# Scan layer in another order on four engines, and an attention stage that looks for shares before the turned rows

## The reference

```python
x = L0_attn_x
xn = _layernorm(x)
x = x + attention(xn) * _silu(expert_choice_ffn(xn))      # 32 experts, 8 tokens each per batch
xn = _layernorm(x)
# selective scan, 512 channels, 16 states
xc, z = split((xn @ fc1_w.T + fc1_b) @ in_proj_w.T)
u = _silu(causal_conv4(xc) + conv_b)
dt_low, Bm, Cm = split(u @ x_proj_w.T)
dt = softplus(dt_low @ dt_proj_w.T + dt_proj_b)
def step(hstate, t):
    dA = jnp.exp(dt_t[..., None] * A)
    hstate = dA * hstate + (dt_t * u_t)[..., None] * B_t[:, None, :]
    y_t = jnp.einsum('bdn,bn->bd', hstate, C_t)
    return (hstate, y_t)
s = ((y + u * D) * _silu(z)) @ out_proj_w.T @ fc2_w.T + fc2_b
# gated network, hidden 768, weights whole numbers over 127
g = _silu((_silu(xn @ wg.T) * (xn @ wu.T)) @ wd.T)
return x + s * g
```

## Time and profile before

| | |
|---|---|
| median of three runs | 2787.99 us (2785.57 to 2789.45) |
| the profiled execution, its own time | 2788.2 us |
| its span, first to last instruction | 2786.4 us |
| mean granted TensorE clock | 0.966 |
| busy in the span | PE 2542.0, DVE 2333.8, ACT 2011.2, POOL 2013.2 us |
| scan layer, start to start of a tile's first step input | 107.4, then 13 times 116.0 to 116.3, then 115.3 us |

### The profile page before, as it was taken

One profiled execution on the slowest core, in us unless ns is written; L12 is line 12 of the kernel. 1 busy time (PEld: TensorE's weight loads), 2 busy tenths in 40 slices (PEclk: granted clock), 3 DMA queues, 4 the chain that ended last, 5 costly groups with the idle time before them and its releaser, 6 DMA issues. The chain is left out here.

```text
span 2786.4 us, 37406 instructions
## 1 busy us (share of the span) xinstructions
PE 2542.0 (91%) x13454; PEld 1490.8 (54%) x13454; DVE 2333.8 (84%) x2899; ACT 2011.2 (72%) x3253; POOL 2013.2 (72%) x682
## 2 busy tenths in 40 slices
PE   7897899999976799999999999999999999999988
PEld 3454344443443465656656566565655656556565
DVE  7685777777733899898998989989899898998996
ACT  4222466666643798897988979889798897988974
POOL 0656011111211999999999999999999999999996
PEclk9898999999978799999999999999999999999999
DMA  6337999888541231321313213132131321313210
GB/s 188 116 116 179 260 218 236 205 200 224 211 161 49 105 130 29 117 92 46 130 26 119 92 46 130 25 120 92 46 130 24 121 92 46 130 24 114 92 46 8
DMA packets 121586, 316.00 MB, mean 113 GB/s; under 512 B 15517, under 2 KB 76445, under 8 KB 104878
## 3 DMA queue, kind: packets, MB, share of 16 engines
q1 hardware_dynamic: 91210, 233.32, 27.3%
q0 software_dynamic: 27888, 79.24, 10.3%
q10 hardware_dynamic: 2304, 1.05, 0.2%
HBM read 278.89 MB, written 43.13 MB: 116 GB/s over the span
## 5 line engine op out<-in xcount | busy, mean ns | idle before, releaser
L1523 DVE TENSOR_TENSOR_SCAN l_st<-l_p_a,l_hl,l_st 128x512 f32<-128x512 f32 x768 | 930.2, 1263 | 90.5 <-ACT l_p_a L1808 83.3
L1721 POOL TENSOR_TENSOR l_st<-l_st,lw_cs 128x2048 f32<-128x2048 f32 x192 | 878.4, 4634 | 3.2 <-ACT l_hl L1813 3.2
L1808 ACT ACTIVATE l_p_a<-l_dt,lw_a_neg 128x512 f32<-128x512 f32 x1024 | 666.5, 681 | 67.2 <-DVE keep_xg L1523 41.1
L1713 POOL TENSOR_TENSOR l_st<-l_bs,l_dtu 128x2048 f32<-128x2048 f32 (+1 forms) x128 | 555.1, 4337 | 57.2 <-PE l_p_y L2098 53.3
L2098 PEld LDWEIGHTS l_p_y<-keep_ident,l_st 128*128 128x128 f32 x3072 | 355.1, 145 | 118.6 <-issue 73.0
L2098 PE MATMUL l_p_y<-keep_ident,l_st 128*128 128x128 f32 x3072 | 380.5, 281 | 28.7 <-POOL l_st L1721 28.7
L1020 ACT ACTIVATE a_pr<-a_p_s 128x512 f32<-128x512 f32 x512 | 284.7, 596 | 143.8 <-PE a_p_s L1089 140.0
L931 DVE TENSOR_REDUCE a_mpart<-a_p_m 128x1 f32<-128x512 f32 x512 | 312.0, 679 | 12.2 <-PE a_p_m L1045 11.0
L1523 DVE TENSOR_TENSOR_SCAN keep_xg<-l_p_a,l_hl,keep_xg 128x512 f32<-128x512 f32 x256 | 314.5, 1265 | 1.6
L1721 POOL TENSOR_TENSOR keep_xg<-keep_xg,lw_cs 128x2048 f32<-128x2048 f32 x64 | 299.7, 4682 | 2.0 <-ACT l_hl L1813 2.0
L858 POOL DMA_DIRECT2D a_w<-in_w_dram x32 | 23.1, 737 | 327.2 <-PE a_p_m L1119 271.3
(11 more groups left out here) (246 smaller groups left out, 4007.9 us busy)
## 6 DMA issues: line engine op xcount, KB each, us to landing
l_bs<-s_bc SPq DMA_DIRECT2D x64, 1024.0 KB, 4.7
lw_cs<-s_bc SPq DMA_DIRECT2D x64, 1024.0 KB, 4.7
a_w<-in_w_dram POOLq DMA_DIRECT2D x32, 1024.0 KB, 12.0
late<-in_w_dram POOLq DMA_DIRECT2D x32, 1024.0 KB, 19.4
kx<-s_kp SPq DMA_DIRECT2D x96, 256.0 KB, 12.3
s_kp<-late SPq DMA_DIRECT2D x96, 128.0 KB, 2.1
s_vp<-late SPq DMA_DIRECT2D x16, 544.0 KB, 3.5
a_vg<-s_vp SPq DMA_DIRECT2D x16, 544.0 KB, 14.8
```

The source lines that it names most:

```text
L1523: eng.tensor_tensor_scan(st[k % NG][:, n, :], p_a[:, n, :], st[k % NG][:, n, :], hl[:, k, n:n + 1], ALU.mult, ALU.add).then_inc(scan_ok, 1)
L1713: eng.tensor_tensor(st[n][:, first:NG, :], bs[:, 4 * n + first:4 * n + 4, :], dtu[(k // NG) % 2][:, :].unsqueeze(1).broadcast_to([P, NG - ...
L1721: eng.tensor_tensor(st[n][:, :, :], st[n][:, :, :], cs[:, 4 * n:4 * n + 4, :], ALU.mult).then_inc(cm_ok, 1)
L1808: eng.activation(p_a[:, n, :], dt[c % 2][:, :], ACT.Exp, scale=a_neg[:, c, m:m + 1]).then_inc(dA_ok, 1)
```

## The change

**Attention.** The call of `one_choice` moves in front of the wait for the turned rows, still behind the maxima.

```diff
                     maxima(g, b, hg)
+                    if g == HG:
+                        eng.wait_ge(consts, 16 * 4)
+                    if g >= HG:
+                        one_choice(g - HG, b - 1, hg)
                     if hg % 2:
                         eng.wait_ge(hTp_ok, q + 1)
...
                     if g == 0:
                         return
-                    if g == HG:
-                        eng.wait_ge(consts, 16 * 4)
-                    if g >= HG:
-                        one_choice(g - HG, b - 1, hg)
                     take(*prev(g, b, hg))
```

```diff
-                 ("op", 0, END, 0), ("dt", 2, SCAN, 1), ("op", 1, END, 1), ("cv", 0, FRONT, 0), ("z", 0, SCAN, 1),
...
+        FILLS = (("tr", 1, FRONT, 1), ("dn", 1, END, 0), ("yb", 3, END, 1), ("xc", 0, FRONT, 0), ("op", 0, END, 1),
+                 ("xc", 1, FRONT, 0), ("z", 0, SCAN, 1), ("dt", 2, SCAN, 0), ("z", 1, SCAN, 0), ("op", 1, END, 1),
```

GpSimd:

```diff
                     if end:
+                        weighed(f, 11)
+                        weighed(f, 12)
                         dbu(f, 15)
+                        weighed(f, 13)
                     if scan:
                         step_input(s, o, 0)
...
                     if scan:
+                        weighed(s, 0)
                         step_input(s, o, 1)
-                        weighed(s, 0)
                         dbu(s, 3)
                         weighed(s, 1)
                         weighed(s, 2)
                         dbu(s, 5)
                         weighed(s, 3)
-                        step_input(s, o, 2)
-                    if end and f < NT - 1:
-                        residual(f)
-                    if scan:
                         weighed(s, 4)
                         dbu(s, 7)
                         weighed(s, 5)
+                        step_input(s, o, 2)
+                    if end:
+                        residual(f)
+                    if scan:
+                        dbu(s, 9)
                         weighed(s, 6)
-                        dbu(s, 9)
                         weighed(s, 7)
```

TensorE's and ScalarE's ends of a period, and the first tile:

```diff
-                    if q == 0:
-                        keep_busy(12, p_w[:, 0, :])
...
+                        up_h(q, s, o, 3)
+                        up_h(q, s, o, 4)
+                        sums(s, 14)
+                        up_h(q, s, o, 5)
+                    if front:
+                        step_low(q, q, 1)
+                    if scan:
+                        down(q, s, 0)
+                        sums(s, 15)
+                    if nxt:
+                        turn(q, q + 1, 0)
```

```diff
                     if front:
                         step_input(q, 0)
                     if scan:
-                        exp_unit(s, 15, 2)
+                        gate_z(s, 3)
+                        gate_h(s, 5)
+                    if nxt:
+                        normed(q + 1)
+                    if scan:
+                        exp_tables()
                         exp_unit(s, 15, 3)
                     if front:
                         exp_unit(q, 0, 0)
                         exp_unit(q, 0, 1)
-                    if scan:
-                        gate_z(s, 3)
-                    if front:
-                        exp_tables()
                         exp_unit(q, 0, 2)
+                        exp_unit(q, 0, 3)
```

More of the change, by code:

```diff
@@ L1506, in first_conv @@
                     taken(eng, "tr", 0, 1)
-                    wait(eng, done["cv"], c - 1)
+                    wait(eng, done["cv"], max([x + 1 for x in range(c) if bank("cv", x) == bank("cv", c)], default=0))
                     taken(eng, "xc", 0, c)
@@ L1911, in period @@
                         step_log(s, 1)
+                        exp_unit(s, 1, 0)
                         exp_unit(s, 1, 1)
+                        last(s, 0)
                         exp_unit(s, 1, 2)
                         exp_unit(s, 1, 3)
+                    if end:
+                        gate_out(f, 0)
                     if front:
@@ L1968, in period @@
                         exp_unit(s, 6, 2)
-                        step_input(s, 2)
-                        last(s, 5)
                         exp_unit(s, 6, 3)
                         exp_unit(s, 7, 0)
+                        last(s, 5)
+                        summed(s, 0)
+                        exp_unit(s, 7, 1)
+                    if front:
+                        conv_out(q, p, 0)
+                    if scan:
+                        exp_tables()
+                        exp_unit(s, 7, 2)
+                        exp_unit(s, 7, 3)
+                        step_log(s, 3)
+                        step_input(s, 2)
                     if front:
@@ L2050, in period @@
                         exp_unit(s, 14, 3)
+                        last(s, 13)
+                    if front:
+                        step_log(q, 0)
+                    if q == 0:
+                        norm_scale(1)
+                    if scan:
                         gate_h(s, 4)
-                        last(s, 13)
-                        gate_h(s, 5)
-                        summed(s, 2)
-                        gate_z(s, 2)
                         exp_tables()
@@ L2228, in period @@
                     if end:
+                        back(q, f, p, 3)
+                    if front:
+                        conv_in(q, q, p, 0)
+                    if scan:
+                        sums(s, 1)
+                    if end:
                         mix(q, f, p, 0)
+                    if front:
+                        conv_in(q, q, p, 1)
                     if scan:
+                        gate_z(q, s, o, 0)
                         step_low(q, s, 2)
-                        sums(s, 1)
                         sums(s, 2)
+                        gate_z(q, s, o, 1)
+                        sums(s, 3)
                     if end:
@@ L2238, in period @@
                     if scan:
-                        gate_z(q, s, o, 0)
-                        sums(s, 3)
-                        gate_z(q, s, o, 1)
+                        sums(s, 4)
+                        step_low(q, s, 3)
                     if front:
                         conv_in(q, q, p, 2)
+                    if scan:
+                        sums(s, 5)
+                    if front:
                         conv_out(q, q, 1)
-                    if scan:
-                        sums(s, 4)
-                    if front:
                         conv_out(q, q, 2)
@@ L2268, in period @@
                     if scan:
+                        sums(s, 9)
                         gate_h(q, s, o, 2)
-                        up_h(q, s, o, 1)
-                        sums(s, 9)
+                        back(q, s, o, 1)
+                        sums(s, 10)
+                        gate_z(q, s, o, 2)
+                        gate_h(q, s, o, 3)
+                        sums(s, 11)
+                        up_h(q, s, o, 2)
+                        back(q, s, o, 2)
                     if q == 0:
```

295 lines of the change are left out of this document (119 added, 176 removed).

## The result

| | before | after |
|---|---|---|
| median of four runs | 2787.39 us (2785.57 to 2789.45) | 2760.84 us (2758.17 to 2762.53) |
| ratio | | 0.9906, interval 0.9894 to 0.9919 |
| span of the profiled execution | 2786.4 us | 2758.0 us |
| mean granted TensorE clock | 0.966 | 0.973 |

The account below looks back on a forecast made before the run. GpSimd was taken to bound the scan layer, 112.31 us busy in a period of 116.20. Terms 11.7 + 14 + 0 - 2.4 = 23.3 us off 2788.0 gave 2765; range 2740 to 2789, the forecast's own 2755 to 2774.

Parts of the forecast that it names:

- five passes, bias to copy: Attention passes 5 to 13: the choice fits into VectorE's 9.14 us wait, giving 2.33 us a pass, 11.7 us together.
- pass 15: Attention's pass 15: it has no scores behind it and gives nothing.
- 14 steady periods: Scan layer: a period of 115.2 instead of 116.2 us, 1.0 gained in each, 14 us together.
- head: First scan period and first tile: up to 3.5 us gained against up to 3 lost, taken as 0.
- tail: Program's end: 1.5 us between the mixes and about 0.9 for the last down-projection, 2.4 lost; bounds 0 and 5.
- the six waits: GpSimd's waits in a steady period at weighed(4), weighed(15), weighed(0) and drives 9, 11, 13, added up to 2.9 us.
- The floor: Rival, scan layer: GpSimd's small waits vanish, a period of 113.4 us, about 2740 in all; chance 0.14.
- Nothing from the scan layer: Rival: VectorE or TensorE late at new places, the period stays 116.2 us, only attention gains, about 2779; chance 0.17.
- Low clock without slack: Rival, scan periods: a low-clock stretch in chains with 0.3 of slack costs 1.6 us a period, about 2787; chance 0.11.
- Sums 5 missing the gap: Rival, in front of drive 9: TensorE's sums 5 come late and GpSimd stands, 3.3 us a period, about 2807; chance 0.07.
- Dearer table switches: Rival, chain to weighed(15): two table loads each 1.3 us longer than the rows' 1.30, about 2801; chance 0.01.

Follow-up runs that it names:

- e1_choice: The kernel before with only the attention part of the change, one_choice in front of the wait for the turned rows: 2770.33 us, ratio 0.9938.
- e2_scan: The changed kernel with one_choice put back behind the bias, the scan layer's part alone: 2778.51 us, ratio 0.9965.
- e3_normed: The changed kernel with ScalarE's normed(q+1) moved from in front of exponential 15,3 to behind last(15): 2759.15 us, ratio 0.9897.
- e7_last4: As e6_gates, with ScalarE's last(4) moved in front of exponentials 5,1 to 5,3: 2748.92 us, ratio 0.9862.
- e8_ends: The changed kernel with the first tile's old ScalarE order and twelve warming matmuls restored and the last tile's second mix in bank 0: 2756.74 us.
- e6_gates: As e3_normed, with gate_z(3) and gate_h(5) in front of step_input(q, 0) and hidden(5) behind scan 0,1: 2747.64 us, ratio 0.9854.
- e4_pool_plus: The changed kernel with one more GpSimd product of 128x512 behind drive 13 in each scan period: 2779.37 us, ratio 0.9970.

## Why the prediction was right, and where it wasn't

Forecast 2765, measured 2760.84. The terms:

| term | predicted | measured |
|---|---|---|
| five passes, bias to copy | 11.7 | 11.7, and 3.1 of low clock in passes 7 and 11 |
| in front of them | 0 | 0.3 |
| pass 15 | 0 | 3.85, low clock |
| 14 steady periods | 14 | 16.6 |
| head | 0 | 0.4 (-2.05 and 2.42) |
| tail | -2.4 | -7.5 (-3.80, -1.79, -1.92) |
| sum | 23.3 | 28.4 (26.6 in the medians) |

The time came out within 4 us, and that is in part luck: 7.3 us in attention that weren't in the sum stand against 5.1 us too little taken off for the tail.

- **Attention.** "A pass gives 11.00 - 8.67 = 2.33" held in each of the five; TensorE's 1.66 is gone and no choice stands behind the bias. Left out was the clock: two of the passes had taken 1.5 more before, and e1_choice and e2_scan show that this goes with the wait. "Pass 15 has no scores behind it and gives nothing" is right for the order; its 3.85 us are the length of a low-clock stretch, and e3_normed, with the same instructions, had 30.54 us there.
- **Steady period.** 114.94 instead of 115.2. Of the six waits, weighed(4) was 0.69 (0.6 predicted), weighed(15) 0.68 (0.7), weighed(0) 0.34 (0.3), drive 11 0.36 (0.3), drive 13 0.55 (0.7), and drive 9 had none (0.3). Its reason: the residual's issue took 1.31 us before drive 9 could start, not 0.81, and the 0.5 that the earlier trace rows show on the next instruction (5.07 instead of 4.54) were not there. Gate 1 waited 0.94 (1), up 3 1.07 (1.4), mixed(0) held VectorE 0.79 and not 2.5. The step that was wrong in kind is the adding up: e3_normed took away a wait of 0.68 and gained 0.12, e7_last4 took away 0.92 and gained nothing. The sum came out because all the waits were estimated, not because each of them counts. "One stretch a period is at the lower clock now" is true of the period that I read, and of seven of the 14.
- **Head.** The sum 0 held, out of two parts of opposite sign. VectorE waited 1.77 before the fourth convolution (1.7 predicted), and 2.9 of the 3.5 us of waits at `weighed(0)` went. Not seen: drive 9's 3.20.
- **Tail.** The wrong term, outside its bounds of 0 to 5. The mixes' gap was foreseen (1.5; it is 1.61, and 1.85 in the last stretch, which e8_ends gave back). I had looked at the last period alone. The same bank clash is in the one before it, where the convolution input that stands between mix 0 and gate 0 is missing, and `weighed(15)` waited 1.59 at the end. The row to read would have been GpSimd's last tile before: not one wait in it, so every chain made longer costs there.
- **Rivals.** The floor: e6_gates came to 114.05, and no kernel to 113.4. Nothing from the scan layer: e2_scan alone is 9.6 us under before. Low clock without slack: the steady periods have no such stretch, the first scan period has; e4_pool_plus had three, at 1.1 us each and not 1.6. Sums 5 missing the gap: once, 3.2 us, and from a late TensorE as described. Dearer table switches: in the chain to `weighed(15)` the wait is the 0.68 that a load at 1.30 us gives; nothing of the second figure of the Trainium skill (ScalarE: Activation LUTs, What ACT_TABLE_LOAD costs) is seen.

## What to carry over

Work that nobody waits for belongs in the bottleneck pair's common wait; what it gives is read from a repetition of the loop that doesn't have the work. Waits of the bounding engine that hang on one chain count once: shorten the chain, then see which wait is left, as `normed` gave nothing until `gate_z(3)` and `hidden(5)` followed it. A periodic order has to be walked again for the periods where a part is missing, since bank neighbours and idle time are others there.

## What the hardware showed

- A VectorE product with both inputs in SBUF took 3.42 us on average beside GpSimd and ended 0.55 us behind GpSimd's instruction in 32 cases of 32; with one input in PSUM it took 0.67. Two of the former cost 4.7 us in the period without a low-clock stretch and 6.3 or 7.9 in those with one or two.
- A low-clock stretch (one group of sums 0.8 to 1.7 us longer) cost nothing in a period of the kernel before (116.2 us with it and without) and 1.1 us in each of three places in e4_pool_plus.
- The same instructions behind the same 3.14 us of idle TensorE ran for one to five groups at the lower clock: 25.23 to 30.54 us in the executions here. Twenty-two matmuls in the gap (2.57 us) kept the higher clock to the end of the pass, in three executions of three.
- The accumulating DMA's issue on GpSimd takes 1.3 us either way: 0.81 with the next 128x2048 products ending 0.5 later, up to GpSimd's next wait (before), or 1.31 with the next 128x1024 one at its normal 2.38.
